# Graph attention on one core: the four tiles of a bank are summed by TensorE in PSUM at offsets read from memory, instead of being added one by one by VectorE

## The chip, the cores and the metric

One core of a Trainium2 chip. The metric is the device time in microseconds (us); lower is better. The kernel before was timed three times.

## The reference

A graph of 12,500 nodes (N) and 412,500 edges (E), sorted by destination. Two layers follow each other:

```python
# layer 0: weighted sum over neighbours, two matrices, layernorm
rel = segment_sum(x[src] * weight[:, None], dst); x = layernorm(x + rel @ W1 + (rel * x) @ W2)
# layer 1: attention over the incoming edges, 8 heads of 16 lanes
q, k, v = x @ Wq + bq, x @ Wk + bk, x @ Wv + bv;  e = edge_attr @ We + be
logits = ((q[dst] * k[src]).sum(-1) + (q[dst] * e).sum(-1)) * SCALE
attn = segment_softmax(logits, dst)
out = segment_sum(attn[..., None] * v[src], dst);  x = layernorm(x + out @ Wo + bo)
```

## The kernel before

It runs in five parts, one after the other: preparation (`prepare`), the neighbour sum of layer 0 (`neighbours`, 403 steps of 1,024 edges), the projections by node (`nodes_one`), the attention (`attention`), and the output by node (`nodes_two`). The change is nearly all in `attention`.

`attention` walks over 202 groups of 2,048 edges: 16 tiles of 128 edges, handled as four banks (k = 0 to 3) of four tiles (s = 0 to 3). In the kernel before, tile `s * 4 + k` belongs to bank k. Since edges are sorted by destination, a tile touches a window of at most 128 consecutive nodes. For a group the steps are:

- GpSimd (POOL) gathers the key and value rows of the sources, 16 indirect DMAs (L1058), into a ring of three groups; it waits for `msg_ready` of three groups ago. SyncE (SP) loads edge attributes, relative positions, eight windows of queries at a time (`load_q`, L1031), and the words that name them (`load_cols`).
- TensorE (PE) transposes attributes (`attr_fill`, L1082) and keys (`keys`, L1102, with the product by We, L1106), spreads the queries over their edges with a one-hot matrix `pick` (`q_fill`, L1091), and sums query times key by head (`logits`, L1115).
- VectorE (DVE) makes `pick`, multiplies (`products`, L1215), and finds each row's softmax peak by scans: `scan_forward`, `scan_back`, `place_ends`, then PE `gather_ends`, DVE `carry_over`, PE `spread_carry`, DVE `row_inflow` and `row_peaks`, PE `spread_drop`, ScalarE (ACT) `exponents`, PE `turn_weight`, ACT `weight_copy`, and last DVE `messages` (weight times value, L1280).
- ACT makes the one-hot matrix `put` (`put_masks`, L1393 and L1396), copies query banks and attributes out of PSUM (`q_drain` L1384, `attr_drain` L1378), and issues the five small DMAs of `load_words` and `load_marks`.
- PE's `out_bank` multiplies messages and weights by `put`: eight products, four with 8 weight columns into the partitions `s*32` to `s*32+7` (L1146, the softmax denominators), four with 128 columns (L1149). Each tile has its own 128 columns of `out_ps`, so the windows stay apart.
- DVE's `add_bank` loads four window starts from memory into registers and adds the four tiles' results into the accumulator `acc` (128 x 2 x N in SBUF) one after the other, since windows overlap (L1298). `out_bank` of the next bank waits for the last of them. `carry_decay` scales the one column of `acc` that the group shares with the one before.

The order of each engine is written out by hand in a `body` that works on three groups at once: c (output), n = c+1 (softmax) and m = c+2 (queries and keys). It is unrolled over three groups inside a hardware loop.

## Time and profile before

| | |
|---|---|
| median of 3 runs | 10865.19 us |
| lowest and highest | 10864.79 and 10868.03 us |
| span of the profiled execution | 13260.2 us |
| PE, weight loads, DVE, ACT, POOL busy in it | 7727.7, 6102.5, 5558.1, 3368.4, 8204.5 us |
| mean granted TensorE clock | 0.725 |

The profile gives the span from the first to the last instruction of the profiled execution, 13260.2 us; it gives no other time for that execution. The timed executions took 2,395 us less than this span, so durations of single instructions and what ends a wait are to be read from the profile, and the pace of a stage is to be taken from it with care. An engine's row says when an instruction started, how long it took, and in brackets how long the engine was idle before it and what ended that.

### The profile page before, as it was taken

The numbers are of one execution on the slowest core, as the hardware profiler recorded it, in microseconds if no ns is written. First come the engines' busy times: TensorE is split into PE (matmuls) and PEld (weight loads), VectorE is DVE, ScalarE is ACT, GpSimd is POOL, SyncE is SP. The second block draws the span as 40 slices with busy tenths as digits, with TensorE's granted clock in tenths as the row PEclk, the third lists the DMA queues.
The fourth block names the chain that finished last, engine by engine and source line by source line (L and its number), as shares of the span: only waits on it lengthen the run. The fifth ranks groups of instructions, "written<-read, shape, count | busy, mean of one in ns | idle before, by whom it ended". The sixth has DMA issues, their size and how long they took to land. (4 is left out here: it accounts for less than half of the span.)

```text
span 13260.2 us, 210680 instructions
## 1 busy us (share of the span) xinstructions
PE 7727.7 (58%) x48566; PEld 6102.5 (46%) x48566; DVE 5558.1 (42%) x20556; ACT 3368.4 (25%) x7806; POOL 8204.5 (62%) x6569
## 2 busy tenths in 40 slices
PE   2444444444444444444577777777777777777777
PEld 1344333334344334333355555555555555555555
DVE  2333333333333333334544444444444454444455
ACT  1111111111111111111233333333333333333333
POOL 3888888888888888886344444444444444444441
PEclk7666666666666666666777777777777777777776
DMA  8666666666666666666555555555555555555552
GB/s 197 106 106 106 106 105 106 106 105 106 106 106 106 106 106 106 106 106 130 182 137 138 139 137 138 136 140 140 138 137 138 138 139 139 140 137 138 137 138 76
DMA packets 2236565, 1660.60 MB, mean 125 GB/s; under 512 B 734074, under 2 KB 1994684, under 8 KB 2236252
## 3 DMA queue, kind: packets, MB, share of 16 engines
q0 software_dynamic: 628992, 668.10, 30.1%
q1 hardware_dynamic: 1538069, 907.12, 24.7%
q10 hardware_dynamic: 69448, 84.72, 1.9%
q8 instruction: 24, 0.39, 0.0%
q14 instruction: 32, 0.26, 0.0%
HBM read 1374.49 MB, written 284.45 MB: 125 GB/s over the span
## 5 line engine op out<-in xcount | busy, mean ns | idle before, releaser
L467 POOL DMA_INDIRECT rel_sum<-sums,row x3224 | 5004.5, 1552 | 1193.1 <-issue 631.8
L1058 POOL DMA_INDIRECT kv<-kv_rows,src_idx x3232 | 3121.7, 966 | 3420.8 <-DVE msg L1280 2494.2
L423 PE MATMUL coef_ps<-same,spread 128*128 128x128 f32 x6448 | 1640.6, 437 | 3528.6 <-DVE spread L396 2914.6
L423 PEld LDWEIGHTS coef_ps<-same,spread 128*128 128x128 f32 x6448 | 1424.2, 325 | 3711.0 <-DVE spread L396 3078.8
L1298 DVE TENSOR_TENSOR acc<-acc,out_ps 128x256 f32 x3232 | 1364.4, 422 | 1946.9 <-remote 911.2
L410 DVE TENSOR_TENSOR row<-moved,src_col 128x8 int32<-128x8 f32 x403 | 69.5, 173 | 3760.8 <-DMA rel_sum<-sums,row 3760.7
L1091 PE MATMUL ring_ps<-pick,q_win 128*128 128x128 f32 x6464 | 1265.6, 351 | 141.6 <-issue 134.3
L1091 PEld LDWEIGHTS ring_ps<-pick,q_win 128*128 128x128 f32 x6464 | 1075.8, 249 | 583.2 <-issue 574.4
L1149 PE MATMUL out_ps<-put,msg 128*128 128x128 f32 x6464 | 1236.2, 350 | 3.8 <-issue 3.8
L396 DVE TENSOR_SCALAR spread<-iota_n,rel_col,w_col 128x128 f32<-128x128 f32 x3224 | 1214.5, 382 | 0.0
L392 DVE SCALAR_TENSOR_TENSOR same<-src_bc,src_col,later 128x128 f32<-128x128 f32 x3224 | 1118.2, 347 | 202.0 <-issue 136.5
L1149 PEld LDWEIGHTS out_ps<-put,msg 128*128 128x128 f32 x6464 | 1054.8, 248 | 260.9 <-issue 260.9
L451 ACT ACTIVATE sums<-sum_ps 128x512 f32<-128x512 f32 x806 | 437.6, 594 | 2864.6 <-DMA rel_sum<-sums,row 2862.4
L1393 ACT ACTIVATE put<-iota_n,at_neg_rel 128x128 f32<-128x128 f32 x3232 | 1028.0, 390 | 471.1 <-PE out_ps L1149 336.9
L1115 PE MATMUL logit_ps<-prod,head_in 128*32 128x128 f32 x6464 | 604.2, 327 | 886.1 <-issue 523.5
L445 ACT ACTIVATE coef<-coef_ps 128x512 f32<-128x512 f32 x806 | 481.3, 597 | 2312.0 <-PE coef_ps L423 2307.6
L432 PEld LDWEIGHTS sum_ps<-x_win,coef 128*128 128x128 f32 x6448 | 1000.9, 243 | 0.0
L432 PE MATMUL sum_ps<-x_win,coef 128*128 128x128 f32 x6448 | 1000.8, 321 | 0.0
L1384 ACT ACTIVATE q_edge<-ring_ps 128x512 f32<-128x512 f32 x808 | 479.3, 593 | 1934.7 <-remote 1317.3
L1215 DVE TENSOR_TENSOR prod<-ke_ps,q_edge 128x512 f32<-128x512 f32 x808 | 551.3, 682 | 757.7 <-issue 683.5
L1115 PEld LDWEIGHTS logit_ps<-prod,head_in 128*32 128x32 f32 x6464 | 234.7, 119 | 1102.5 <-issue 672.2
L1378 ACT ACTIVATE attr_t<-ring_ps 128x512 f32<-128x512 f32 x404 | 241.2, 597 | 1714.4 <-remote 1692.7
(164 smaller groups left out, 7310.4 us busy)
## 6 DMA issues: line engine op xcount, KB each, us to landing
q_win<-q_rows SPq DMA_DIRECT2D x3232, 64.0 KB
src_bc<-src_flat SPq DMA_DIRECT2D x403, 512.0 KB
x_win<-in_x SPq DMA_DIRECT2D x3224, 64.0 KB
rel<-rel_flat SPq DMA_DIRECT2D x404, 256.0 KB
attr<-in_edge_attr SPq DMA_DIRECT2D x804, 128.0 KB
mark<-marks ACTq DMA_DIRECT2D x202, 256.0 KB
kv<-kv_rows,src_idx POOLq DMA_INDIRECT x3232
rel_sum<-sums,row POOLq DMA_INDIRECT x3224
```

The lines of the kernel that those rows point to most:

```text
L392: nc.vector.scalar_tensor_tensor(out=same[:, b, j, :], in0=src_bc[:, b, j * P:(j + 1) * P], scalar=src_col[:, t], in1=later[:], op0=ALU.is ...
L396: nc.vector.tensor_scalar(spread[:, b, j, :], iota_n[:], rel_col[:, t], w_col[:, t], ALU.is_equal, ALU.mult).then_inc(masks, 1)
L423: last = nc.tensor.matmul(coef_ps[k][:, i, :], spread[:, b, j, :], same[:, b, j, :], start=True, stop=True)
L432: last = nc.tensor.matmul(sum_ps[k][:, i, :], coef[:, b, j, :], x_win[:, b, j, :], start=True, stop=True)
L467: pool.indirect_dma_start(out=rel_sum[r], out_offset=bass.IndirectOffsetOnAxis(ap=row[:, b, j:j + 1], axis=0), in_=sums[:, b, j, :], in_of ...
L1058: pool.indirect_dma_start(out=kv[:, 2 * i + u, k * S + s, :], out_offset=None, in_=kv_rows, in_offset=bass.IndirectOffsetOnAxis(ap=src_idx ...
L1091: mm = nc.tensor.matmul(to[:, s, :], q_win[:, u, k % 2 * S + s, :], pick[:, k % 2, s, :], start=True, stop=True)
L1115: mm = nc.tensor.matmul(logit_ps[s * Q:(s + 1) * Q, :], head_in[:, k, :], prod[:, k % 2, s, :], start=(k == 0), stop=(k == B - 1))
L1149: mm = nc.tensor.matmul(out_ps[:, 0, s, :], msg[:, k % 2, s, :], put[:, k % 2, s, :], start=True, stop=True)
L1215: nc.vector.tensor_tensor(prod[:, k % 2], ke_ps[k % 2][:], q_edge[:, k % 2], ALU.mult).then_inc(prod_ready[k], 1)
L1298: nc.vector.tensor_tensor(win, win, out_ps[:, :, s, :], ALU.add).then_inc(summed[k][s], 1)
L1393: nc.scalar.activation(put[:, k % 2, s, :], iota_n[:], ACT.Abs, bias=neg_rel[:, i, j:j + 1]).then_inc(put_dist, 1)
```

## The change

The tiles of a bank are now consecutive (tile `k * 4 + s`), so that a bank covers one window of at most 512 nodes. PE first writes zeros over both halves of `out_ps` with two products of a blank bf16 matrix, then adds the four tiles' products into `out_ps` at column offsets that it loads from memory into registers. The offsets (`offs`) are made once by DVE during the neighbour sum. The denominators of the four tiles now all go to partitions 0 to 7. DVE adds only the first column of the result to `acc` (shared with the bank before) and copies the other 511 columns of the denominators; ACT copies the 511 columns of the messages. So `add_bank` is gone, and `keep_bank` (DVE) and `keep_out` (ACT) are new. Messages overwrite the values in the kv ring, and the gathers wait for `out_done` instead of `msg_ready`. `load_words` and `load_marks` move from ACT's queue to SP's; the marks take four DMAs instead of one. Every engine's body has a new order.

```diff
@@ preparation
-                nc.vector.tensor_scalar(rel_t[:], nrel_t[:], -1.0, FAR, ALU.mult, ALU.min).then_inc(vec, 1)
+                nc.vector.tensor_scalar(rel_t[:], nfirst_t, -1.0, FAR, ALU.mult, ALU.min).then_inc(vec, 1)
-                    for i, a in enumerate((srcf_t, nrel_t, w_t)):
+                    for i, a in enumerate((srcf_t, nrel_t, w_t, nfirst_t)):
-                for i, a in enumerate((src_col, neg_rel, w_col)):
+                for i, a in enumerate((src_col, neg_rel, w_col, neg_first)):
@@ neighbours, once
+                nc.vector.tensor_tensor(off_q[:], first_q[:], first_q[:, :, 0:1].to_broadcast([TP // 32, 8, 4]),
+                                        ALU.subtract).then_inc(offs_ready, 1)
@@ attention, SyncE
+                def load_words(n):
+                    i = n.slot
+                    wait_alone(sp, out_kept[B - 1], n.plus(-3).count(), passed)
+                    wait_alone(sp, den_kept[B - 1], n.plus(-3).count(), passed)
+                    tiles = bass.ds(n.g * A, A)
+                    sp.dma_start(neg_rel[:, i, :], neg_cols[:, tiles]).then_inc(words_in[i], 16)
+                    sp.dma_start(window[:, i, :], firsts[tiles].rearrange("(a t) -> a t", a=1)).then_inc(words_in[i], 16)
+                    sp.dma_start(shift[:, i, :], offs[tiles].rearrange("(a t) -> a t", a=1)).then_inc(words_in[i], 16)
+                def load_marks(n):
+                    b = n.slot
+                    wait_alone(sp, below_ready, n.plus(-3).count(), passed)
+                    tiles = marks[bass.ds(n.g * A, A)].rearrange("(k s) m e -> s k (m e)", s=S)
                     for s in range(S):
+                        sp.dma_start(mark[s * Q:(s + 1) * Q, b, :, :].rearrange("p m e -> p (m e)"),
+                                     tiles[s].rearrange("k (a x) -> k a x", a=1).to_broadcast([B, H, 4 * P])
+                                     ).then_inc(mark_in[b], 16)
@@ GpSimd
-                            wait_alone(pool, msg_ready[1], n.plus(-3).count(2, 1 - u), passed)
+                            wait_alone(pool, out_done[2 * u + 1], n.plus(-3).count(), passed)
@@ TensorE
                 def out_bank(c, k):
-                    pe.wait_ge(msg_ready[k % 2], c.count(2, 1 - k // 2))
-                    pe.wait_ge(put_ready[k % 2], c.count(2, 1 - k // 2))
-                    wait(pe, summed[k - 1][S - 1], c.plus(-(k == 0)).count())
+                    pe.wait_ge(words_in[c.slot], c.landed(48))
+                    pe.sem_inc(passed, 1)
+                    later = load_starts(pe, regs, shift[0:1, c.slot, k * S + 1:(k + 1) * S], SP - P)
+                    wait(pe, out_kept[k - 1], c.plus(-(k == 0)).count())
+                    wait(pe, den_kept[k - 1], c.plus(-(k == 0)).count())
+                    for i in range(2):
+                        nc.tensor.matmul(out_ps[:, 1 - i, :].rearrange("p (s e) -> p s e", e=P), blank[:],
+                                         blank[:].rearrange("p (a e) -> p a e", a=1).to_broadcast([P, S, P]),
+                                         start=True, stop=True)
+                    pe.wait_ge(msg_ready[k], c.count())
+                    pe.wait_ge(put_ready[k], c.count())
+                    msg = messages_of(c, k)
+                    columns = [slice(0, P)] + [bass.ds(at, P) for at in later]
                     for s in range(S):
                         lanes = slice(s * Q + k * H, s * Q + (k + 1) * H)
-                        nc.tensor.matmul(out_ps[s * Q:s * Q + H, 1, s, :], weight[:, c.slot, lanes], put[:, k % 2, s, :],
-                                         start=True, stop=True)
+                        nc.tensor.matmul(out_ps[0:H, 1, columns[s]], weight[:, c.slot, lanes],
+                                         put[:, k % 2, s, :], start=False, stop=True, skip_group_check=True)
                     for s in range(S):
-                        mm = nc.tensor.matmul(out_ps[:, 0, s, :], msg[:, k % 2, s, :], put[:, k % 2, s, :],
-                                              start=True, stop=True)
+                        mm = nc.tensor.matmul(out_ps[:, 0, columns[s]], msg[:, s, :], put[:, k % 2, s, :],
+                                              start=False, stop=True, skip_group_check=True)
@@ VectorE
-                def add_bank(c, k):
-                    start = load_starts(dve, regs, tiles, LAST)
-                    dve.wait_ge(out_done[k], c.count())
-                    for s in range(S):
-                        win = acc[:, :, bass.ds(start[s], P)]
-                        nc.vector.tensor_tensor(win, win, out_ps[:, :, s, :], ALU.add).then_inc(summed[k][s], 1)
+                def keep_bank(c, k):
+                    first = first_of(c, k)
+                    dve.wait_ge(out_done[k], c.count())
+                    column = acc[:, :, bass.ds(first, 1)]
+                    nc.vector.tensor_tensor(column, column, out_ps[:, :, 0:1], ALU.add).then_inc(joined, 1)
+                    nc.vector.tensor_copy(acc[:, 1, bass.ds(first + 1, SP - 1)], out_ps[:, 1, 1:SP]
+                                          ).then_inc(den_kept[k], 1)
@@ ScalarE
-                def load_words(n):
-                def load_marks(n):
+                def keep_out(c, k):
+                    first, = load_starts(act, first_reg, window[0:1, c.slot, k * S:k * S + 1], N)
+                    act.wait_ge(joined, c.count(B, B - 1 - k))
+                    nc.scalar.activation(acc[:, 0, bass.ds(first + 1, SP - 1)], out_ps[:, 0, 1:SP], ACT.Copy
+                                         ).then_inc(out_kept[k], 1)
```

The new orders, with c, n, m as above (`place_ends` to `scan_back` and so on are the steps named before):

```text
PE : keys(n,1) q_fill(n,3) logits(n,1) out_bank(c,1) logits(n,2) logits(n,3) attr_fill(m,0) out_bank(c,2)
     gather_ends(n) spread_carry(n) q_fill(m,0) spread_drop(n) out_bank(c,3) q_fill(m,1) turn_weight(n)
     keys(m,0) attr_fill(m,1) out_bank(n,0) q_fill(m,2) logits(m,0)
DVE: place_ends(n) messages(c,3) keep_bank(c,2) carry_over(n) picks(m,0) row_inflow(n) row_peaks(n) picks(m,1)
     keep_bank(c,3) messages(n,0) picks(m,2) products(m,0) carry_decay(n) messages(n,1) products(m,1) picks(m,3)
     keep_bank(n,0) messages(n,2) products(m,2) products(m,3) keep_bank(n,1) scan_forward(m) scan_back(m)
ACT: q_drain(n,3) keep_out(c,1) put_masks(c,3) keep_out(c,2) put_masks(n,0) attr_drain(m,0) q_drain(m,0)
     exponents(n) weight_copy(n) q_drain(m,1) keep_out(c,3) put_masks(n,1) attr_drain(m,1) put_masks(n,2)
     q_drain(m,2) keep_out(n,0)
```

## Rows read from the trace of the kernel before

**Rows 1.** Busy time by engine, clock and DMA in stretches of the span (view by windows).

```profile
core 0: us, PE busy (x) PEld busy (x) DVE busy (x) ACT busy (x) POOL busy (x), PEclk, DMA share, GB/s
13007.30:13027.30 20.00, 16.98 (x168) 12.68 (x167) 15.69 (x43) 11.22 (x29) 0.00 (x0) 1.00 0.14 41
...
13055.00:13260.00 205.00, 160.12 (x582) 121.12 (x582) 103.52 (x386) 75.54 (x153) 13.63 (x25) 0.62 0.21 65
0.00:212.00 212.00, 23.35 (x114) 17.02 (x115) 53.26 (x74) 18.49 (x83) 2.13 (x7) 0.69 1.00 240
212.00:6199.00 5987.00, 2554.30 (x12862) 2372.32 (x12860) 1945.12 (x10836) 916.91 (x1609) 5003.03 (x3224) 0.67 0.63 106
6473.00:13055.00 6582.00, 4827.15 (x34106) 3474.58 (x34106) 3240.41 (x8675) 2309.64 (x5858) 3121.75 (x3232) 0.78 0.51 137
```

**Rows 2.** Timeline of POOL, one indirect DMA of each of the two loops.

```profile
6197.12 1.55 POOL L467 DMA_INDIRECT rel_sum<-sums,row  x1 [0.30 <-issue]
...
6475.83 0.95 POOL L1058 DMA_INDIRECT kv<-kv_rows,src_idx  x1 [0.30 <-issue]
```

**Rows 3.** Timeline, the first and the last `place_ends` of the 202 groups.

```profile
6547.79 0.19 DVE L1237 TENSOR_TENSOR ends<-row_tile,swept 128x32 f32<-128x32 f32 x1
...
13035.65 0.19 DVE L1237 TENSOR_TENSOR ends<-row_tile,swept 128x32 f32<-128x32 f32 x1
```

**Rows 4.** Timeline in the middle of the attention, 9013 to 9019 us.

```profile
9013.70 0.60 PE L1082 MATMUL ring_ps<-ident,attr 128*128 128x128 f32 x4
...
9018.49 0.74 PE L1115 MATMUL logit_ps<-prod,head_in 128*32 128x128 f32 x7 [1.03 <-issue]
...
9018.75 0.60 ACT L1378 ACTIVATE attr_t<-ring_ps 128x512 f32<-128x512 f32 x1 [3.85 <-remote]
9018.79 2.08 DVE L1298 TENSOR_TENSOR acc<-acc,out_ps 128x256 f32 x4 [1.35 <-remote]
```

**Rows 5.** Timeline of DVE in the third group from the end.

```profile
13003.36 1.29 DVE L1280 TENSOR_TENSOR msg<-kv,weight 128x512 f32<-128x512 f32 x2
...
13007.11 2.08 DVE L1298 TENSOR_TENSOR acc<-acc,out_ps 128x256 f32 x4 [2.39 <-PE out_ps L1149]
13009.20 0.69 DVE L1215 TENSOR_TENSOR prod<-ke_ps,q_edge 128x512 f32<-128x512 f32 x1
...
13019.21 0.23 DVE L1245 TENSOR_TENSOR_SCAN carry<-whole_row,carry,misc_ps 8x16 f32<-8x16 f32 x1
...
13020.43 0.15 DVE L1253 CUSTOM_DVE_ANT_0 scrap<-misc_ps,row_tile 128x16 f32<-128x16 f32 x1
...
13021.50 0.21 DVE L1270 SCALAR_TENSOR_TENSOR drop<-carry,mark,peak 8x1 f32<-8x1 f32 x1
...
13025.34 1.28 DVE L1280 TENSOR_TENSOR msg<-kv,weight 128x512 f32<-128x512 f32 x2
13026.54 0.15 DVE L1307 TENSOR_TENSOR acc<-acc,decay 128x2 f32 x1
13027.70 0.42 DVE L1298 TENSOR_TENSOR acc<-acc,out_ps 128x256 f32 x1 [1.01 <-PE out_ps L1149]
```

**Rows 6.** Timeline of PE in the same group; ends of matmuls are modelled, starts are recorded.

```profile
13009.10 1.16 PE L1091 MATMUL ring_ps<-pick,q_win 128*128 128x128 f32 x8
13010.19 0.41 PE L1146 MATMUL out_ps<-put,weight 128*8 128x128 f32 x8
13010.53 1.16 PE L1149 MATMUL out_ps<-put,msg 128*128 128x128 f32 x8
13011.52 0.60 PE L1082 MATMUL ring_ps<-ident,attr 128*128 128x128 f32 x4
...
13017.68 1.13 PE L1106 MATMUL ke_ps<-attr_t,we 64*128 64x512 f32 x4
13018.74 1.16 PE L1091 MATMUL ring_ps<-pick,q_win 128*128 128x128 f32 x8
```

**Rows 7.** Timeline of ACT's and SP's part in the same group.

```profile
13010.78 0.60 ACT L1384 ACTIVATE q_edge<-ring_ps 128x512 f32<-128x512 f32 x1 [1.77 <-PE ring_ps L1091]
...
13012.63 5.02 SPq L1031 DMA_DIRECT2D q_win<-q_rows  x8
```

More of the change, by code:

```diff
@@ L955, in _ @@
                                         ).then_inc(c_b, 1)
[L956 to L957 removed]
+                nc.vector.memset(blank[:], 0.0).then_inc(c_b, 1)
                 dve.wait_ge(const_ready, 2)
@@ L1044, in _ @@
                 load_cols(Group(0, 1))
-                groups(sp, NG, HEAD, TAIL, {1: range(-2, 3), 2: (-4, -2, 0)}, ((16 * U, 0), (16 * U, 1), (32, 1)), body)
+                groups(sp, NG, HEAD, TAIL, body)
             @block.gpsimd
@@ L1074, in attr_fill @@
                     full = n.is_under(NG - 1)
-                    loads = 2 if full else sum(LAST_ROW + (s * B + 2 * u + h) * P < E for s in range(S) for h in range(2))
+                    loads = 2 if full else sum(LAST_ROW + ((2 * u + h) * S + s) * P < E for s in range(S) for h in range(2))
                     if full:
@@ L1156, in body @@
                     if mid:
-                        q_fill(n, 2)
-                    if old:
-                        out_bank(c, 0)
-                    if mid:
                         keys(n, 1)
                         q_fill(n, 3)
+                        logits(n, 1)
                     if old:
                         out_bank(c, 1)
-                    if new:
-                        attr_fill(m, 0)
                     if mid:
@@ L1170, in body @@
                     if new:
-                        q_fill(m, 0)
+                        attr_fill(m, 0)
                     if old:
@@ L1175, in body @@
                         gather_ends(n)
+                        spread_carry(n)
                     if new:
-                        keys(m, 0)
-                        q_fill(m, 1)
+                        q_fill(m, 0)
                     if mid:
-                        spread_carry(n)
+                        spread_drop(n)
                     if old:
@@ L1183, in body @@
                     if new:
+                        q_fill(m, 1)
+                    if mid:
+                        turn_weight(n)
+                    if new:
+                        keys(m, 0)
                         attr_fill(m, 1)
                     if mid:
-                        spread_drop(n)
+                        out_bank(n, 0)
                     if new:
+                        q_fill(m, 2)
                         logits(m, 0)
-                        logits(m, 1)
-                    if mid:
-                        turn_weight(n)
                 body(Group(0, -2))
                 body(Group(0, -1))
-                groups(pe, NG, HEAD, TAIL, {1: range(6), 2: range(1, 11), 32: range(96, 161, 32),
-                                            16 * U: range(32 * U, 80 * U + 1, 16 * U)}, ((16 * U, 1), (16 * U, 2)), body)
+                groups(pe, NG, HEAD, TAIL, body)
             @block.vector
             def _(dve):
-                regs = [dve.alloc_register(f"window{j}") for j in range(S)]
                 first_reg = [dve.alloc_register("first_node")]
@@ L1344, in body @@
                     if new:
+                        picks(m, 1)
+                    if old:
+                        keep_bank(c, 3)
+                    if mid:
+                        messages(n, 0)
+                    if new:
+                        picks(m, 2)
+                        products(m, 0)
+                    if mid:
+                        carry_decay(n)
+                        messages(n, 1)
+                    if new:
                         products(m, 1)
                         picks(m, 3)
-                    if old:
-                        add_bank(c, 3)
@@ L1349, in body @@
                     if mid:
-                        messages(n, 0)
+                        keep_bank(n, 0)
+                        messages(n, 2)
+                    if new:
+                        products(m, 2)
+                        products(m, 3)
+                    if mid:
+                        keep_bank(n, 1)
+                    if new:
+                        scan_forward(m)
+                        scan_back(m)
                 body(Group(0, -2))
                 body(Group(0, -1))
-                groups(dve, NG, HEAD, TAIL, {1: range(6), 2: (4, 6, 8)}, ((32, 1), (32, 2), (48, 1)), body)
+                groups(dve, NG, HEAD, TAIL, body)
```

346 lines of the change are left out of this document (178 added, 168 removed).

## The prediction, made before the kernel ran

> **What bounds the kernel now.** I read the windows first, cut by stage. Preparation takes 212 us, the neighbour sum 5,987, the attention 6,582 and the last part 205 [rows 1]; what is left, 274 us from 6199 to 6473, is the projections. In the neighbour sum POOL is never free: each of 3,224 scatters takes 1.55 us with 0.30 before it [rows 2], 1.85 x 3,224 = 5,964 us. The change does not touch that.
>
> The attention needs care, since the timed runs are 2,395 us shorter than the span. Between the first and the last `place_ends` lie 13035.65 - 6547.79 = 6,488 us for 201 periods [rows 3], 32.3 us a group. But in the middle of it whole engines stand still together: the attribute transposes start at 9013.70, last 0.60, and the ACT copy that waits for them starts at 9018.75; DVE resumes at 9018.79, within 0.04 us, and PE has just come out of a gap of 1.03 that no operation explains [rows 4]. I take that for the weight of recording, not for the kernel. Two things give the pace without it. First the sum: all outside the 201 periods is 212 + 5,987 + 274 + 75 (6473 to 6548) + 19 (13036 to 13055) + 205 = 6,772 us. 10,865 - 6,772 = 4,093, over 201 = 20.4 us a group. Second, the third group from the end, where nearly no DMA runs (DMA share 0.14): the pair of `messages` starts at 13003.36 and again at 13025.34, 21.98 us [rows 5]. In it DVE waited 2.39 us for the first output bank, against 1.01 a group later, at the full clock; less 1.38 it is 20.6. The two agree, so I take 20.6 a group (201 x 0.2 = 40 us is the gap between them), and the sums below are differences against the 10,865 of the timed runs; against the profiled span they cannot be made.
>
> Three engines are near those 20.6 us. DVE is busy 15.69 of 20.0 us, in an unbroken order with waits for output banks [rows 1, 5]: it sets the pace. PE is busy 16.98 of 20.0 [rows 1]. POOL needs 16 x (0.95 + 0.30) = 20.0 us for its gathers [rows 2]: a floor that the change leaves in place. So at most 0.6 us a group, 120 us in all, can be won, whatever DVE is relieved of.
>
> **The change part by part.**
>
> *DVE.* Sixteen window adds go: four of 2.08 us, 8.3 us as they stand in the order [rows 5]. In come four column adds like the decay (0.15) and four copies of 128x511 from PSUM; the copy has no row of its own and I take it between ACT's 0.60 [rows 7] and the product's 0.69 [rows 5]: 4 x (0.15 + 0.65) = 3.2 us. DVE falls by 5 us a group. That gain can only be had down to POOL's 20.0.
>
> *ACT.* Four copies of 0.60 [rows 7] come in, 2.4 us on top of 11.22 of 20 [rows 1]; five DMA issues leave. It stays under 15 us and is not late.
>
> *PE, denominators.* Four products with 8 columns each (L1146) take 0.34 us until the next burst starts, four with 128 columns (L1149) take 0.99 [rows 6], though both move the same 4 x 128 columns. The first four run side by side, since each writes its own strip of 32 partitions; in the new kernel all write partitions 0 to 7 and can only follow each other. Bounds: 0.34 (nothing lost) and 0.99; I take 0.95, as what moves is the same and only the weights are narrower. That is 4 x 0.6 = 2.4 us. The Trainium skill (TensorE: Matmul & The Clock Gate, section "Part 3: Packing small matmuls — row/col tiling") says that products in different column groups run at once and that the output's start partition picks the group; it speaks against this edit. By that rule, the trace agrees: 0.34 against 0.99.
>
> *PE, blanks.* Eight bf16 products of 512 columns a group. No bf16 product is in the trace. A float32 tile of 128 columns is two records, 0.99 / 4 = 0.25 us; a pair of float32 products of 512 columns, side by side, takes 1.06 [rows 6]. So a blank lies between 0.12 (one record of the first) and 0.53 (half of the pair); one with a single pass is nearest to the 128-column tile that takes several, so 0.25, and 8 x 0.25 = 2.0 us. The skill (same page, "Back-to-back issue gap") has the only price: 0.216 us when warm, with which this term would be 1.7 us.
>
> *PE, sum.* The busy time of a group was 16.98 us; it becomes 16.98 + 2.4 + 2.0 = 21.4 us, at a clock that stays at 2.4 GHz (1.00 over the 20 us with this density [rows 1]). That alone is above the 20.6 of today.
>
> *PE, waits that the new order leaves.* (a) `gather_ends` is followed at once by `spread_carry`. Between them DVE must see bank 2 done, add (0.15), copy (0.65), and scan (0.23 + 0.15, from 19.21 on [rows 5]); with two handovers, 1.4 us of idle PE. Before, `keys` and `q_fill` lay there. (b) From `spread_carry` to `spread_drop` DVE needs 20.43 to 21.71, 1.3 us [rows 5], after picks; `q_fill` covers 1.05, 0.5 stays. (c) The blanks of a bank wait for both copies of the bank before: in `out_bank(c,2)` the two logits and `attr_fill` lie between, about 1.1 us against 0.15 + 0.65 + handovers: 0.1. So 21.4 + 2.0 = 23.4 us.
>
> *PE, registers.* Four times a group PE loads three words before the blanks, and twenty-four matmuls a group take their column from a register. I take nothing: in the new order 1 to 4 us of matmuls lie ahead of each load, and I assume that PE's sequencer runs ahead of the array while they are worked off. Bounds: nothing below, and above the 2.4 us from the end of `q_fill` (13009.10 + 1.16) to SP's first query DMA (13012.63), which holds a load of eight words and other issues [rows 6, 7].
>
> *SP.* Its DMAs go from 24 to 32 a group. Eight query loads take 5.02 us [rows 7], 0.63 each: 15.1 becomes 20.1 us. Just covered by 23.4, late if the rest were faster.
>
> *POOL.* It now waits for `out_done` instead of `msg_ready`, one out burst later. The ring holds three groups, and from a release to the use lie some 1.5 groups (35 us) against 10 us of gathers. Nothing.
>
> *Outside the groups.* Preparation gets 26 transposes and 26 small ACT copies and one subtraction, before the scans that wait for neighbour rows in any case, and loses one cast. Nothing, with 10 us either way.
>
> Sum: 23.4 - 20.6 = 2.8 us x 201 = 563 us; 10,865 + 563 = 11,430 us, slower by 5%.
>
> **The rivals.**
>
> 1. *DVE's relief is what counts (faster).* PE has slack that I count as busy: its bursts hold gaps of 0.1 to 0.2 us (0.99 for four tiles, of which the modelled busy time is more), which may close when the queue is full. If denominators and blanks cost under 1.5 us instead of 4.4 and the idle of (a) and (b) is filled, PE fits in 20 us and POOL sets the pace: 20.1 to 20.3 us, 10,865 - 201 x 0.4 = about 10,785. It decides from a PE total under 20.4. For it: DVE's order is the unbroken one today. Against: 0.34 against 0.99.
> 2. *The registers are exposed (slower still).* If each load costs PE 1.2 us (half the upper bound), 4.8 us a group: 28.2, + 965 more, 12,395. One of four exposed gives 11,670. Against: waits on PE stand in its queue.
> 3. *SP becomes the bound.* Marks come late, and scans wait at the end of DVE's body. At 0.63 a DMA SP needs 20.1, so it would only bite near POOL's floor: 20.4 to 21.0, 10,865 to 10,985.
> 4. *The gain and loss cancel*, no change.
>
> **How the numbers follow.** The forecast, PE as bound with 21.3 to 25 us, has 0.62; registers 0.12; SP or a milder PE, slower by 20 to 140 us, 0.07; no change within 0.2% (22 us, about what a measurement can tell) 0.05; the faster case 0.14. The range reaches to 10,790 below, near the faster case, and to 11,850 above (25.5 us a group: blanks at 0.53 give 8 x 0.28 = 2.2 us more), leaving out most of the registers' case. Alone the forecast has 11,050 to 11,800.
>
> **What would show it.** In the profile after: L1146's successor with 8 records over 0.9 us instead of 0.34; a burst of blanks before each; PE busy above 21 us a group in a stretch without stalls, near the end of the attention; DVE with idle time before the column adds, ended by PE; POOL waiting for `out_done` in the groups near the end. The forecast is wrong if DVE's order is still unbroken, if PE idles before blanks for a register load, or if POOL runs without waits.

## The result and the profile after

The changed kernel takes 11,688.93 us (median of 4 runs, 11,685.99 to 11,692.43) against 10,864.99 of the kernel before: ratio 1.0757, 95% interval 1.0742 to 1.0773, that is 824 us slower. The forecast was 11,430 in a range of 10,790 to 11,850. The direction and the engine that bounds the changed kernel were right; the size was 259 us short. Where some executions of a kernel below ran slower at a lower mean clock than its others (one of four of e11, two of four of e12), the ratio and its interval are those of the faster ones alone.

Here the profiled execution (span 11,684.1 us) takes as long as the timed ones, so its rows can be used as they stand. The windows of the kernel after, over the neighbour sum and over all groups (window, length, busy time and instructions of PE, weight loads, DVE, ACT, POOL, granted clock, DMA share, GB/s):

```profile
212.00:6199.00 5987.00, 2540.33 (x12854) 2366.14 (x12852) 1941.58 (x10827) 915.81 (x1607) 5000.91 (x3223) 0.67 0.63 106
6473.00:11485.00 5012.00, 4552.42 (x35715) 3169.85 (x35715) 2584.30 (x7063) 2627.14 (x6663) 3224.80 (x3222) 0.98 0.70 180
```

In the window of the neighbour sum every engine has the busy time and the instructions of before to within 0.6% [rows 1]: the difference is in the attention. The first and last `place_ends` (start, duration):

```profile
6493.84 0.19 DVE L1314 TENSOR_TENSOR ends<-row_tile,swept 128x32 f32<-128x32 f32 x1
11460.61 0.19 DVE L1314 TENSOR_TENSOR ends<-row_tile,swept 128x32 f32<-128x32 f32 x1
```

4,966.8 us over 201 periods are 24.71 us a group, and 11,689 - 4,967 = 6,722 us lie outside. These 6,722 us serve for every kernel below: its time less 6,722, over 201, is its group. The first and last `place_ends` in the traces of the kernels below agree with this to 0.1 us a group. The kernel before then has 20.6. PE is busy 4,552 / 201 = 22.6 us a group. PE's instructions in one group, from the products of `out_bank(n,0)` to the same place a group later (24.34 us), with the part that the change made:

```profile
9000.94 1.04 PE L1227 MATMUL out_ps<-put,weight 128*8 128x128 f32 x8
...
9011.84 0.59 PE L1218 MATMUL out_ps<-blank 128*128 128x512 bf16 x2 [0.24 <-issue]
9012.36 1.04 PE L1227 MATMUL out_ps<-put,weight 128*8 128x128 f32 x8
9013.33 1.16 PE L1230 MATMUL out_ps<-put,kv 128*128 128x128 f32 x8
9014.42 0.23 PE L1194 MATMUL misc_ps<-ends,row_head 128*8 128x32 f32 x2
9015.73 0.41 PE L1198 MATMUL misc_ps<-carry,row_head_t 8*128 8x34 f32 x2 [1.08 <-DVE carry L1324]
9016.11 1.16 PE L1162 MATMUL ring_ps<-pick,q_win 128*128 128x128 f32 x8
9017.52 0.38 PE L1203 MATMUL misc_ps<-drop,head_of_t 8*128 8x1 f32 x2 [0.25 <-DVE drop L1347]
9017.76 0.36 PE L1204 MATMUL misc_ps<-drop,den_of_t 8*128 8x1 f32 x2
9018.75 0.59 PE L1218 MATMUL out_ps<-blank 128*128 128x512 bf16 x2 [0.62 <-issue]
...
9025.28 0.93 PE L1227 MATMUL out_ps<-put,weight 128*8 128x128 f32 x7
```

From a pair of blanks to the denominators 0.52 us, from these to the messages 0.97 us, where the kernel before had 0.34 [rows 6]. PE stands still for 0.24 + 1.08 + 0.25 + 0.62 = 2.2 us, and its work is 24.34 - 2.2 = 22.1 us. `gather_ends` and `spread_carry` stand one behind the other with 1.08 us between them, and 0.25 us lie before `spread_drop`. The gaps of 0.24 and 0.62 us stand before blanks, where the register load is, with the waits for the words and for the copies of the bank before; e3 and e6 below show that it is the load.

Three of the waits for PE in the 4,000 us from 7000 to 11000 (total, times, longest), the last row that of SP's queue:

```profile
DVE acc L1385 <- PE out_ps L1230: 1249.6, 646, 5.1
POOL kv L1127 <- PE out_ps L1230: 680.7, 322, 3.3
SPq L83 <- PE ring_ps L1162: 393.4, 197, 3.1
```

VectorE's unbroken order [rows 5] is gone. VectorE, POOL and SP all wait for PE, but SP's wait is only 393.4 us in the 162 groups of this stretch, 2.4 us a group: its own queue needs 24.7 - 2.4 = 22.3 us.

The group's mean (24.71) is above the 24.34 us shown. Every fourth group lasts 25.9 us, since PE then runs at half clock, 1.2 GHz, for 3 to 4 us behind its waits:

```profile
9064.40 0.41 PE L1198 MATMUL misc_ps<-carry,row_head_t 8*128 8x34 f32 x2 [1.08 <-issue]
...
9068.25 1.87 PE L1227 MATMUL out_ps<-put,weight 128*8 128x128 f32 x8
```

The same products take 1.04 us at 2.4 GHz (9012.36). This costs 0.37 us a group on average.

### The profile page after: what moved, and what is told of

Its sections match the earlier page's. It is cut to its first block and busy times, and to the rows that moved or that the text cites. A ratio compares the mean times of both kernels' runs of the same rounds, so it can differ in the third digit from the quotient of the medians.

```text
span 11684.1 us, 226052 instructions
## 1 busy us (share of the span) xinstructions
PE 7447.1 (64%) x50208; PEld 5799.5 (50%) x50208; DVE 4893.2 (42%) x18943; ACT 3691.3 (32%) x8640; POOL 8316.0 (71%) x6569
## 5 line engine op out<-in xcount | busy, mean ns | idle before, releaser
L1127 POOL DMA_INDIRECT kv<-kv_rows,src_idx x3232 | 3234.5, 1001 | 1742.3 <-issue 911.4
L1230 PE MATMUL out_ps<-put,kv 128*128 128x128 f32 x6464 | 960.9, 293 | 0.0
L1162 PE MATMUL ring_ps<-pick,q_win 128*128 128x128 f32 x6464 | 897.9, 282 | 6.3 <-DMA q_win<-q_rows 6.0
L1230 PEld LDWEIGHTS out_ps<-put,kv 128*128 128x128 f32 x6464 | 807.0, 196 | 186.9 <-issue 186.9
L1227 PE MATMUL out_ps<-put,weight 128*8 128x128 f32 x6464 | 883.3, 282 | 0.0
L1162 PEld LDWEIGHTS ring_ps<-pick,q_win 128*128 128x128 f32 x6464 | 787.3, 192 | 178.8 <-issue 153.9
L1385 DVE TENSOR_TENSOR acc<-acc,out_ps 128x2 f32 x808 | 127.7, 158 | 1568.7 <-PE out_ps L1230 1568.7
L1227 PEld LDWEIGHTS out_ps<-put,weight 128*8 128x8 f32 x6464 | 529.0, 92 | 465.2 <-issue 354.1
L1477 ACT ACTIVATE acc<-out_ps 128x511 f32 x808 | 482.1, 597 | 875.4 <-DVE acc L1385 868.7
L1218 PE MATMUL out_ps<-blank 128*128 128x512 bf16 x1616 | 494.0, 388 | 180.8 <-issue 173.7
```

What stands on the lines that cost most here:

```text
L1127: pool.indirect_dma_start(out=kv[:, 2 * i + u, j, :], out_offset=None, in_=kv_rows, in_offset=bass.IndirectOffsetOnAxis(ap=src_idx[:, i, t ...
L1162: mm = nc.tensor.matmul(to[:, s, :], q_win[:, u, k % 2 * S + s, :], pick[:, k % 2, s, :], start=True, stop=True)
L1218: nc.tensor.matmul(out_ps[:, 1 - i, :].rearrange("p (s e) -> p s e", e=P), blank[:], blank[:].rearrange("p (a e) -> p a e", a=1).to_broadc ...
L1227: nc.tensor.matmul(out_ps[0:H, 1, columns[s]], weight[:, c.slot, lanes], put[:, k % 2, s, :], start=False, stop=True, skip_group_check=True)
L1230: mm = nc.tensor.matmul(out_ps[:, 0, columns[s]], msg[:, s, :], put[:, k % 2, s, :], start=False, stop=True, skip_group_check=True)
```

## The experiments

**Theory.** PE's added work and waits set the pace; each term can be taken off by itself. **Rivals:** the register addresses cost the most; SP's longer queue costs it; VectorE's relief was never worth anything.

### TensorE's terms, one by one

`e1_den_strips` (the sum of the denominators is left out; the last part takes a maximum with 1 for the reciprocal):

```diff
-nc.tensor.matmul(out_ps[0:H, 1, columns[s]], weight[:, c.slot, lanes],
+nc.tensor.matmul(out_ps[s * Q:s * Q + H, 1, s * P:(s + 1) * P], weight[:, c.slot, lanes],
```

> The changed kernel, but the four denominator products of a bank go to four different strips of 32 partitions and to fixed columns, so that they can run side by side again; this leaves out the right columns of the denominators, and the last part takes a maximum in place of their reciprocal. My theory (PE's own work in its order sets the pace, 24.7 us a group): the four take 0.34 us instead of 0.97, 4 x 0.63 = 2.5 us a group less, 201 groups, so 11,689 - 507 = about 11,180. Rival A (PE waits for register loads and handovers, its array work is not the bound): the array's work shrinks but the waits grow by as much, 11,650 to 11,690. Rival B (SP's queue of 32 DMAs is the bound): unchanged, 11,690.

`e2_no_blanks`: the first product of each bank starts it, the others add to it or write where nothing stands yet; `out_ps` is zeroed once, at the start of the attention:

```diff
-for i in range(2):
-    nc.tensor.matmul(out_ps[:, 1 - i, :]..., blank[:], ..., start=True, stop=True)
-nc.tensor.matmul(out_ps[:, 0, columns[s]], msg[:, s, :], put[:, k % 2, s, :], start=False, ...)
+nc.tensor.matmul(out_ps[:, 0, columns[s]], msg[:, s, :], put[:, k % 2, s, :], start=(s == 0), ...)
```

> The changed kernel without the two blank products of each bank: the first of the four products of either half starts the sum, and out_ps is zeroed once at the start. My theory: from the first blank to the first denominator product lie 0.53 us in the trace, 4 x 0.53 = 2.1 us a group, about 11,260. Rival A: the blanks lie in time that PE waits for messages and masks anyway, 11,650 to 11,690. Rival B: 11,690.

`e3_early_load`: the wait for the words and the register load of bank 3 stand ahead of `spread_drop`:

```diff
+if old:
+    later = offsets(c, 3)
 if mid:
     spread_drop(n)
 if old:
-    out_bank(c, 3)
+    out_bank(c, 3, later)
```

> The changed kernel with the offsets of bank 3 loaded before the products of spread_drop instead of behind them. My theory: of the four loads of a group only this one is exposed, 0.62 us, so 201 x 0.62 = 125 less, about 11,565. Rival A (register work is exposed at all four banks, this is a quarter of it): also about 11,565, told apart by the run with fixed columns. Rival B: 11,690.

`e6_static` (the four tiles go to fixed columns, so their windows are not summed, and PE neither waits for the words nor loads them; the last part as in e1):

```diff
-later = load_starts(pe, regs, shift[0:1, c.slot, k * S + 1:(k + 1) * S], SP - P)
-columns = [slice(0, P)] + [bass.ds(at, P) for at in later]
+columns = [slice(s * P, (s + 1) * P) for s in range(S)]
```

> The changed kernel with fixed column offsets in out_ps: no register load and no register in any matmul of PE; this leaves out the right columns of the sums, and the last part takes a maximum in place of the reciprocal. My theory: registers cost 0.62 us at bank 3 and 0.24 at bank 2, all else is hidden, 201 x 0.86 = 173 less, about 11,515. Rival A (registers are the main term): 4 x 1.2 us a group, 965 less, about 10,725. Rival B: 11,690.

`e8_double_blanks` (each pair of blanks is issued twice):

```diff
-for i in range(2):
+for i in (0, 1, 0, 1):
     nc.tensor.matmul(out_ps[:, 1 - i, :]..., blank[:], ..., start=True, stop=True)
```

> The changed kernel with every pair of blank products issued twice. Theory (TensorE sets the pace, and a blank costs its 0.26 us wherever the clock is full): 4 x 0.53 = 2.1 us a group more, less the 0.36 us that the present half-clock stretches cost on average, 26.4 to 26.8 us; 6,722 + 201 x 26.4 to 26.8 = 12,030 to 12,110 us, with a granted clock of 1.00 in the groups. Rival (blanks lie half in waits that would be there anyway, which would explain why leaving them out brought only 156 us): the second pair costs as much as the first did, 11,845 us.

| kernel | time, us | ratio to before (interval) | group | clock, 7000 to 11000 | group at full clock | groups with half clock |
|---|---|---|---|---|---|---|
| after | 11,688.9 | 1.0757 (1.0742 to 1.0773) | 24.71 | 0.98 | 24.34 | 36 of 145 |
| e1_den_strips | 11,491.2 | 1.0575 (1.056 to 1.059) | 23.7 | 0.86 | 21.83 | 147 of 151 |
| e2_no_blanks | 11,532.5 | 1.061 (1.0595 to 1.0625) | 23.9 | 0.93 | 22.45 | 124 of 150 |
| e3_early_load | 11,638.5 | 1.071 (1.0695 to 1.0725) | 24.5 | 0.96 | 23.66 | 52 of 147 |
| e6_static | 11,567.6 | 1.0644 (1.0629 to 1.0659) | 24.1 | 0.96 | 23.37 | 63 of 148 |
| e8_double_blanks | 12,203.2 | 1.123 (1.1211 to 1.1249) | 27.3 | 0.94 | 26.07 | 83 of 131 |

The last two columns come from PE's rows of 7000 to 10600, with a group running from one `gather_ends` to the next. A group counts as one with half clock where a burst of eight query-spread or output products lasts over 1.3 us instead of at most 1.16; the column before it is the median of the others.

Each one went the way expected, and each that takes work or a wait off PE brought less time than its rows say. At full clock the savings are there: 2.5, 1.9, 0.7 and 1.0 us a group in e1, e2, e3 and e6. The half clock took 1.5, 1.1, 0.4 and 0.4 us of them back. The rows of e1 show both things at once; they are one group:

```profile
9003.51 0.41 PE L1198 MATMUL misc_ps<-carry,row_head_t 8*128 8x34 f32 x2 [1.08 <-DVE carry L1324]
9003.89 1.89 PE L1162 MATMUL ring_ps<-pick,q_win 128*128 128x128 f32 x8
...
9008.17 2.08 PE L1230 MATMUL out_ps<-put,kv 128*128 128x128 f32 x8
...
9014.53 0.41 PE L1227 MATMUL out_ps<-put,weight 128*8 128x128 f32 x8
9014.86 1.16 PE L1230 MATMUL out_ps<-put,kv 128*128 128x128 f32 x8
...
9027.41 0.41 PE L1198 MATMUL misc_ps<-carry,row_head_t 8*128 8x34 f32 x2 [1.08 <-DVE carry L1324]
```

In strips the denominators take 0.33 us again (9014.53 to 9014.86), 4 x 0.64 = 2.6 us a group cheaper. But the group lasts 9027.41 - 9003.51 = 23.9 us, only 0.4 less than the clean 24.34, because behind the wait of 1.08 us the products run at half clock (query spread 1.89 us for 1.16, messages 2.08 for 1.16), now in nearly every group. e2 shows the same from another place: without blanks its half clock starts in the products of bank 3, behind the register load.

```profile
9015.33 1.87 PE L1225 MATMUL out_ps<-put,weight 128*8 128x128 f32 x8 [0.74 <-issue]
```

e3 settles where the register load lay bare. With the load ahead of `spread_drop` the gap before the blanks of bank 3 is gone:

```profile
9001.69 0.59 PE L1222 MATMUL out_ps<-blank 128*128 128x512 bf16 x2
...
9019.03 0.36 PE L1204 MATMUL misc_ps<-drop,den_of_t 8*128 8x1 f32 x2
9019.32 0.60 PE L1222 MATMUL out_ps<-blank 128*128 128x512 bf16 x2
...
9025.34 0.59 PE L1222 MATMUL out_ps<-blank 128*128 128x512 bf16 x2
```

A clean group is now 9025.34 - 9001.69 = 23.65 us, 0.69 less; the mean fell by only 0.25, and the clock from 0.98 to 0.96. e6, without any load or register address, took 121 us off. In it the blanks of bank 2 too follow `attr_fill` without a gap:

```profile
9018.19 0.66 PE L1153 MATMUL ring_ps<-ident,attr 128*128 128x128 f32 x4
9018.79 0.59 PE L1215 MATMUL out_ps<-blank 128*128 128x512 bf16 x2
```

So the gap of 0.24 us was a register load as well, and all register work together costs 24.34 - 23.37 = 0.97 us at full clock. The expected times of e1 to e6 held the clock constant, and that was their error.

In e8 the doubled blanks cost 2.56 us a group instead of the 2.1 expected at most. At full clock it is only 26.07 - 24.34 = 1.7 us, since the second pair of a bank costs less than the first: four blanks take 0.96 us to the denominators where two took 0.52.

```profile
9012.93 1.03 PE L1218 MATMUL out_ps<-blank 128*128 128x512 bf16 x4
9013.89 1.04 PE L1227 MATMUL out_ps<-put,weight 128*8 128x128 f32 x8
```

The rest is half clock, 1.2 us a group. My expectation that it would vanish with more work fell: the windows give 0.94. So it is not the amount of PE's work alone that decides.

### Does the half clock follow the waits?

`e7_strips_filler` is e1 with three products for nothing where PE waited:

```diff
 def spread_carry(n):
+    for i in range(3):
+        nc.tensor.matmul(ke_ps[i % 2][:], blank[:], ..., start=True, stop=True)
     pe.wait_ge(carry_ready, n.count(2))
```

> The kernel e1_den_strips with three more blank products, into the free key banks, ahead of each spread_carry, where TensorE stood idle for 1.08 us in every group. Work for nothing, 0.8 us of it. Theory (what TensorE saves comes back as half clock, and the half clock begins behind its waits): the stretch at 1.2 GHz that followed the 1.08 us of idle time in every group (query spread 1.89 us in place of 1.06, messages 2.08 in place of 1.16) goes or becomes rare, and a group falls from 23.75 us to 24.35 - 2.5 = 21.9 us or little above; 6,722 + 201 x 21.9 = about 11,130 us, well under the 11,491 of e1_den_strips although the kernel does more. Rival (the lower clock has nothing to do with the idle time, and other engines bound the group once the denominators are cheap): no gain, 11,490 to 11,520, or more where the blanks do not fit in the wait.

11,235.6 us (ratio 1.034, 1.0323 to 1.0357): 256 us faster than e1, with more work. PE at the same place, with the three products for nothing in the first row:

```profile
9009.43 0.82 PE L1198 MATMUL ke_ps<-blank 128*128 128x512 bf16 x3
9010.58 0.41 PE L1202 MATMUL misc_ps<-carry,row_head_t 8*128 8x34 f32 x2 [0.33 <-DVE carry L1328]
9010.96 1.16 PE L1162 MATMUL ring_ps<-pick,q_win 128*128 128x128 f32 x8
```

The query spread takes 1.16 us, the clock over 7000 to 11000 is 0.97 for 0.86. Since nothing else differs, the wait before `spread_carry` is a cause of the half clock in e1. It ended at 22.5 us a group and not at 21.9. At full clock its groups last 21.83 us, as expected and as in the few such groups of e1; but 60 of 161 still have half clock. From 7000 to 11000 PE waited only 7.3 us for query windows, so it is mainly the half clock that holds e7, with SP's pace, which comes next, right under it.

### Is there a second bound?

`e9_order`: no blanks, loads of banks 2 and 3 ahead, and an order that covers PE's waits. `e10_strips_order`: the same, with e1's strips.

```diff
 gather_ends(n)
+later = offsets(c, 3)
+q_fill(m, 0)
 spread_carry(n)
-q_fill(m, 0)
+out_bank(c, 3, later)
 spread_drop(n)
-out_bank(c, 3)
 q_fill(m, 1)
@@ VectorE
+picks(m, 0)
 keep_bank(c, 2)
 carry_over(n)
-picks(m, 0)
```

> The changed kernel without blanks (the first product of each bank starts it), with the register loads of banks 2 and 3 moved ahead, and a new order: picks(m,0) before keep_bank(c,2) on VectorE; on TensorE gather_ends, q_fill(m,0), spread_carry, out_bank(c,3), spread_drop. So the waits of 1.08, 0.25, 0.24 and 0.62 us a group have work over them. Theory (TensorE's work and its waits are the pace): 22.1 - 2.1 = 20.0 us of work and 0.3 to 1.0 of waits, 20.3 to 21.0 us a group at full clock, 10,800 to 10,940 us; with a third of the saving taken back by half clock, as in the two kernels before, 11,000 to 11,200. Rival (waits move and do not go, since DVE, ACT and POOL are tied to TensorE in a ring): 22.5 us or more, above 11,250.

> As e9_order, and the denominators go to four strips of 32 partitions at fixed columns as in the kernel before (their sum is left out; the last part then takes a maximum with 1 in place of the reciprocal). TensorE's work is 20.0 - 2.5 = 17.5 us a group, about that of the kernel before. Theory: POOL's floor of 20.0 us is the next bound, 20.1 to 20.6 us, 10,760 to 10,870; with half clock for part of it up to 11,000. This is what relieving VectorE is worth when TensorE pays nothing for it: 0 to 100 us. Rival (the change costs through something else than TensorE's added work: SP's queue, the ring released a burst later, the order): stays at 21.5 us or more, above 11,040.

11,232.5 us (1.0336, 1.0319 to 1.0354) and 11,222.1 us (1.0329, 1.0312 to 1.0347), both above what the theory allowed: 22.4 us a group for two kernels that differ by 2.5 us in PE's work. What PE waited for in e9, and SP's queue in e10 through one group and at the end of another:

```profile
9036.89 1.13 PE L1164 MATMUL ring_ps<-pick,q_win 128*128 128x128 f32 x8 [2.24 <-DMA q_win<-q_rows]
```

```profile
9045.62 1.18 SPq L1072 DMA_DIRECT2D rel<-rel_flat  x2
9048.23 4.00 SPq L1082 DMA_DIRECT2D q_win<-q_rows  x8
...
9054.48 4.37 SPq L1082 DMA_DIRECT2D q_win<-q_rows  x8
9059.18 0.33 SPq L1089 DMA_DIRECT2D at_neg_rel<-neg_cols  x1
...
9060.49 3.31 SPq L1098 DMA_DIRECT2D mark<-marks  x4
```

```profile
9019.12 0.24 SPq L1049 DMA_DIRECT2D q_start<-firsts  x1
9022.63 1.02 SPq L1056 DMA_DIRECT2D attr<-in_edge_attr  x2
```

Groups of PE without a wait last 20.1 us in e9, then it waits for query windows. In e10 SP has no wait at all from 7000 to 11000, so its own queue is the bound: 22.4 us a group for 32 DMAs. Between the issues lies what the sum of issues does not show. The register load ahead of the query windows is one such place (from 9046.80, the end of `rel`, to 9048.23). The other comes once every three groups, where SP's loop body of three groups ends: 3.3 us between `q_start` and the next `attr` (9019.36 to 9022.63) instead of 0.3. So SP needs 21.2 to 21.5 us for two groups of three and 24.4 to 24.7 for the third; the loop's end costs 1.0 us a group. To see this without the rest of the change:

`e4_before_sp`, the kernel before with only the queue moved and the marks split:

```diff
@@ SyncE
+load_words(n)
+load_marks(n)        # the marks in four DMAs of 32 partitions
@@ ScalarE
-load_words(m)
-load_marks(m)
```

> The kernel before, with load_words and load_marks on SyncE's queue behind the other loads and the marks in four DMAs, as the change has them; nothing else. VectorE, TensorE and the order stay. Theory (SyncE's queue is a bound of its own: in e10_strips_order it issued its 32 DMAs a group without waiting for anything, and a group took 22.4 us): the group goes from 20.4 to about 22.4 us, 10,867 + 201 x 2.0 = about 11,270 us; down to 11,150 if the register handling of this version is shorter. Rival (the prediction's view, 20.1 us of SyncE hidden under the 20.4 of the group; or the 22.4 us of e9_order and e10_strips_order come from another cause, such as the ring released a burst later): no change, 10,850 to 10,890.

11,703.2 us (1.0766, 1.0748 to 1.0784): 836 us slower, twice the 400 expected. The waits for SP's DMAs:

```profile
PE ring_ps L1113 <- DMA q_win<-q_rows: 448.3, 161, 4.1
POOL kv L1080 <- DMA q_start<-starts: 351.2, 105, 4.5
DVE pick L1230 <- DMA rel<-rel_flat: 311.8, 122, 7.1
```

SP waits for nothing here either; PE, POOL and VectorE wait for its DMAs. The group is 24.8 us, not 22.4, since this version spends more on registers ahead of its query loads; SP's rows of e4:

```profile
9018.65 1.19 SPq L1019 DMA_DIRECT2D rel<-rel_flat  x2
9022.47 4.02 SPq L1031 DMA_DIRECT2D q_win<-q_rows  x8
```

2.63 us from the end of `rel` to the first query DMA, where e10 has 1.43; the second query load differs by as much, together 2.4 us. The two versions differ there in how the eight start words lie in memory, side by side in the change and in strides before; no run varies this alone. The simpler tile order thus seems to pay for part of the DMAs that the change adds.

`e11_order_act` is e9 with the words, the last mark and the whole-tile row back on ACT behind `q_drain(n,3)`, 27 DMAs on SP; `e12_strips_order_act` the same with strips:

```diff
@@ SyncE
-for s in range(S):
+for s in range(S - 1):
     sp.dma_start(mark[s * Q:(s + 1) * Q, b, :, :]...)
@@ ScalarE
 q_drain(n, 3)
+load_words(m)
+load_whole(m)        # mark s = 3 and whole_row
 keep_out(c, 1)
```

> e9_order with load_words, the last of the four mark loads and the whole-tile row back on ScalarE's queue (five DMAs), behind q_drain(n,3); SyncE keeps 27. Theory (SyncE's 22.4 us are what holds e7, e9 and e10 at 11,225 to 11,235): SyncE falls to about 19.3 us, TensorE's 20.1 us and POOL's 20.0 are next: 20.2 to 20.6 us a group, 6,722 + 201 x 20.2 to 20.6 = 10,780 to 10,865 us, the first version with the new method that is not slower than the kernel before; with half clock behind remaining waits up to 10,950. Rival (something else than SyncE holds the group at 22.4): 11,200 or more.

> As e11_order_act, and the denominators go to four strips at fixed columns as in e10_strips_order (their sum is left out). TensorE's work is 18.2 us a group at full clock. Theory: only POOL's 20.0 us and SyncE's 19.3 are left: 20.0 to 20.2 us a group, 10,740 to 10,790 us. That is the whole worth of relieving VectorE where TensorE and SyncE pay nothing, and the difference to e11_order_act is what the serial denominators cost once TensorE is near the bound (20 to 100 us). Rival (ring and clock hold it): 10,870 or more.

e11 takes 10,992.6 us (1.0112, 1.0092 to 1.0132; three executions at 10,988 to 10,994 and a mean clock of 0.80, one at 11,289.8 and 0.699), 240 us less than e9, and SP waits again. That confirms SP as the bound of e9. It is the best of the versions that do the whole computation by the new method, and still 125 us slower than the kernel before. It has one new wait, which my placement made: `keep_out(c,1)` stands behind five DMA issues on ACT, and PE waits 1.19 us for it before bank 2.

```profile
9009.64 1.04 PE L1217 MATMUL out_ps<-put,weight 128*8 128x128 f32 x8 [1.19 <-ACT acc L1493]
```

e12 has 4 x 0.64 us less work for PE than e11 and is slower. Its executions lie far apart, at 11,164, 11,260, 11,370 and 11,475 us, with mean clocks of 0.755, 0.745, 0.736 and 0.726. The first two (1.0315, 1.0264 to 1.0367) take 172 and 267 us more than e11. The profiled execution is that of 11,370 us. Windows of e11, then of e12, and rows of e12:

```profile
7000.00:10700.00 3700.00, 3502.56 (x29475) 2625.44 (x29474) 2241.74 (x6102) 2293.59 (x5759) 2760.64 (x2792) 1.00 0.83 211
```

```profile
7000.00:10700.00 3700.00, 3396.03 (x27096) 2589.39 (x27094) 2034.57 (x5610) 2122.92 (x5294) 2581.48 (x2565) 0.82 0.75 194
```

```profile
9002.93 0.41 PE L1217 MATMUL out_ps<-put,weight 128*8 128x128 f32 x8 [1.78 <-ACT acc L1493]
...
9004.83 2.05 PE L1152 MATMUL ring_ps<-pick,q_win 128*128 128x128 f32 x8
...
9026.71 0.41 PE L1217 MATMUL out_ps<-put,weight 128*8 128x128 f32 x8 [1.73 <-ACT acc L1493]
```

In the profiled execution the clock is 0.82 for 1.00, and a group lasts 9026.71 - 9002.93 = 23.8 us: the wait has grown from 1.19 to 1.78 us, and the half clock behind it takes more than the work that was saved. No trace shows the two faster executions; they are slower than e11 too, at a mean clock between that of the profiled one and e11's 0.80. SP waits in e12 (714.6 us of the 3,600 from 7000 on), so its queue is not the bound. e11 itself has its wait of 1.1 to 1.2 us in every group and no half clock, where e1 had half clock in nearly every group behind 1.08 us: a wait of this length alone does not bring it.

### Was VectorE the bound before?

`e5_before_less_adds`, the kernel before with the denominators left out of the window adds (the last part as in e1):

```diff
-win = acc[:, :, bass.ds(start[s], P)]
-nc.vector.tensor_tensor(win, win, out_ps[:, :, s, :], ALU.add)
+win = acc[:, 0, bass.ds(start[s], P)]
+nc.vector.tensor_tensor(win, win, out_ps[:, 0, s, :], ALU.add)
```

> The kernel before, where the sixteen window adds of VectorE take in only the message half of a bank (128 columns in place of 2 x 128; the denominators are left out, and the last part takes a maximum with 1 for the reciprocal). An add of 0.52 us becomes about 0.27 us, so VectorE has some 3 to 4 us less a group. Theory (VectorE's order sets the pace before, with POOL's 20.0 us right under it): 20.05 to 20.2 us a group, 201 x 0.2 to 0.35 = 40 to 70 us less, 10,795 to 10,830. Rival (POOL alone sets the pace, or TensorE's waits do): no change, 10,860 to 10,870. If POOL's floor is not one, 10,500 or less.

10,900.7 us (1.0029, 1.0018 to 1.0041): no gain, a loss of 33 us. An add was busy for 0.289 us instead of 0.422, 2.1 us a group less for VectorE. PE's longest wait, for the gathered rows (7000 to 11000: total, times, longest), and POOL's instructions from 7000 to 10600 (count, busy time and mean of one in ns, idle time before them):

```profile
PE ke_ps L1102 <- DMA kv<-kv_rows,src_idx: 257.7, 281, 3.6
L1058 POOL DMA_INDIRECT kv<-kv_rows,src_idx x2777 | 2754.5, 992 | 846.3 <-issue 846.3
```

POOL waits for nothing but its own issue, and 16 x (0.992 + 0.305) = 20.75 us is the whole group, (10,900.7 - 6,722) / 201 = 20.8. So POOL sets the pace here, within 0.2 us of the 20.6 of the kernel before, and a gather costs 0.99 us on average in full traffic, not the 0.95 of the one that I read in the trace before. Where the 33 us come from stays open.

## Why the prediction was right, and what it mis-sized

**What bounds the kernel before.** Most likely the wrong engine, with the same number. I had VectorE at 20.6 us with POOL's 20.0 right under it. e5 relieves VectorE and gains nothing, so VectorE's work did not set the pace. POOL needs 20.75 us there, with all transfers running, and is the bound that fits the kernel before too; no undisturbed trace of that kernel shows it. The forecast gave VectorE's relief nothing for another reason (PE was to be over both), so this did not move the sum; that was luck. The 20.4 us that the prediction also worked out held 50 us too many outside the groups, from rows of the stalled execution (6,772 for 6,722).

**Denominators** (forecast 2.4 us): 0.97 for 0.34, 4 x 0.63 = 2.5. Right, and e1 shows that four strips bring it back.

**Blanks** (forecast 2.0): 0.52 to 0.54 us a pair, 2.1. Right, at 0.26 us each; the further pair of e8 costs 0.22 each. The prediction's 0.216 us is near that, but it is not the only price in the section of the Trainium skill that it names (TensorE: Matmul & The Clock Gate, section "Back-to-back issue gap"), which gives it for a single product alone. The blanks are not needed either: e2 does the whole sum without them and takes 156 us less. The Trainium skill (PSUM — Partial Sum Buffer, section "The four PSUM rules") says that the first product of an accumulation clears the written bits of its region, and that a later one adds where the bit is set and overwrites where it is not; e2 relies on this, and its time shows only what the blanks cost.

**PE's sum** (forecast 21.4): 22.1 us of work. 0.7 us short, the base of 16.98 us being modelled busy time: 22.1 - 2.5 - 2.1 = 17.5 us.

**Waits of the new order** (forecast 1.4 + 0.5 + 0.1 = 2.0): 1.08 + 0.25 + 0 = 1.3. The places were right. The 0.5 was mis-sized already in the prediction: 1.3 less the 1.05 that `q_fill` covers is 0.25, as measured.

**Registers** (forecast nothing). This step failed: 0.24 + 0.62 = 0.86 us a group, 0.97 by e6. I let PE's sequencer run ahead while matmuls are worked off. For banks 0 and 1 the rows agree, their blanks follow without a gap. But the load of bank 3 stands behind `spread_drop`, which waits until VectorE is done (9017.52), and then only 0.24 + 0.36 us of matmuls cover the load. e3 removed the gap by putting the load ahead of that wait. Why the load of bank 2 is not covered, with 1.5 us of matmuls ahead of it, stays open. Together it is rival 2 at a fifth of its price.

**The clock** (forecast: stays at 2.4 GHz). The second step that failed: 0.37 us a group in the changed kernel, 0.7 to 1.9 us (mean less full-clock group) in e1, e2, e3, e6 and e7, and in e12 more than what was saved. Only e11 kept 2.4 GHz.

Together: 23.4 + 0.7 - 0.7 + 0.9 + 0.4 = 24.7 us, the measured group; the missing 1.3 x 201 = 261 us are the 259 by which the forecast was low. The errors in waits and in work cancel by luck; registers and clock are what was left out.

**SP** (forecast 15.1 to 20.1 us, covered). Covered, as said, by 24.7, but its size is 22.4 us, as 0.63 us for each DMA leaves out register work between them and the 1.0 us of the loop's end. Rival 3 thus had the right mechanism and too low a price (it also started from 20.4 us and not from the 20.6 of the sum): had PE cost nothing, the kernel would still have taken 6,722 + 201 x 22.4 = 11,224 us, 3.3% more than before. e9 and e10 are that case. The Trainium skill (DMA: Bandwidth & Descriptors, section "Issuing engines are not separate DMA queues") says that issuing from several engines saves only the issue time, usually small beside the transfer; here that time was the bound: e11, with five of the DMAs on the other queue, is 240 us faster than e9.

**Rival 1** (faster) can be excluded: it needed PE below 20.4 us, and even there POOL's floor of 20.6 to 20.75 us left nothing to win. Rival 4 (no change) falls with the measured 7.6%.

**What would show it** came true: denominators over 0.9 us, blanks before each bank, PE over 21 us, VectorE and POOL waiting for the output banks. So did one of the signs against it, PE idle before blanks for a register load.

**Open.** When the half clock comes and how long it stays is not settled: e8 has it with more work (0.94), e5 hardly has it (0.99) with PE busy 87% of the time, and e11 not at all (1.00) with a wait of 1.1 to 1.2 us in every group. Whether e11 without its wait of 1.19 us would beat the kernel before was not tried; POOL's 20.6 to 20.75 us put its best at about the time of the kernel before.

## What to carry to other kernels

Before work is moved between engines, take the floor of every engine and every queue from a stretch where that engine waits for nothing, and include what lies between its instructions: three such figures decided this case (POOL 20.75 us, SP 22.4, PE 22.1 of work and 24.7 with its waits and its half clock), and the engine that was relieved was not one of them. A register load belongs ahead of a wait, not behind it. When PE sets the pace, what a saving brings is only known when its waits are known too: fill or remove the wait first, then take work away.

## What the runs showed of the hardware

- Half clock came behind waits of PE of only 0.6 to 1.8 us in an otherwise dense stream (after, e1, e2, e12), but not behind those of 1.1 to 1.2 us in e11. 0.8 us of products for nothing in such a wait saved 256 us (e7 against e1), and 2.5 us less work a group cost 172 to 267 us (e12's two fastest executions against e11).
- A DMA costs SP's queue 0.70 us on average with all that lies between (22.4 us / 32 in e10), while the issue of a query window itself lasts 0.33 and one in a burst of eight takes 0.50 (4.00 us / 8). The end of SP's loop costs 3 us each time.
- A register load on PE's sequencer that stood behind a wait left 0.62 us bare; ahead of the wait it cost nothing that shows (e3).
- The profiled execution of the kernel before was 22% longer than its timed ones; those of all other kernels here were within 0.5% of theirs, also of e5, which has the same queues. I had taken the stall for a weight of recording in general; what made it in that one execution stays open.
